# Output product by 32-row groups, and two sets of moments taken one stage earlier

## Reference, cut to what matters

```python
x = x + 0.5 * ffn(layernorm(x))     # 16 experts, the best 4 of each token, weighted
x = x + attention(layernorm(x))     # 16 heads of width 16, causal
x = x + 0.5 * ffn(layernorm(x))     # the same weights again
# layernorm(x) = (x - mean) / sqrt(var + 1e-5), no scale and no shift
# attention's end: sum over the heads of Z[b,h,s,:] @ WO  (16 x 256)  + 16 * bO
```

## Time and profile before

| what | us |
|---|---|
| median of 3 runs | 1567.58 (1565.57 to 1567.88) |
| the profiled execution, its own time | 1571.9 |
| its span | 1570.2 |
| PE busy | 1417.3 (90%) |
| PE weight loads busy | 960.6 (61%) |
| DVE busy | 1033.5 (66%) |
| ACT busy | 775.6 (49%) |
| POOL busy | 635.4 (40%) |
| mean granted clock of PE | 0.958 of 2.4 GHz |

### The profile page before, as it was taken

One profiled execution on the slowest core, in us unless ns is written; L12 is line 12 of the kernel. 1 busy time (PEld: TensorE's weight loads), 2 busy tenths in 40 slices (PEclk: granted clock), 3 DMA queues, 4 the chain that ended last, 5 costly groups with the idle time before them and its releaser, 6 DMA issues. The chain is left out here.

```text
span 1570.2 us, 32613 instructions
## 1 busy us (share of the span) xinstructions
PE 1417.3 (90%) x9764; PEld 960.6 (61%) x9764; DVE 1033.5 (66%) x2639; ACT 775.6 (49%) x1316; POOL 635.4 (40%) x676
## 2 busy tenths in 40 slices
PE   4899999999957769999999999999598999999997
PEld 3687888888846623333333343333276788888886
DVE  5675636366778768888788688884267564444667
ACT  4312666555125524665566466567351245655530
POOL 3371433766635460232222132222225406176764
PEclk9999999999979967999999999999879999999999
DMA  7741556888316920442334242200131227488873
GB/s 255 238 189 56 185 189 202 259 254 247 88 51 174 228 80 2 63 63 43 42 43 65 37 65 42 42 3 2 41 99 69 95 67 243 151 263 248 251 230 108
DMA packets 159221, 199.08 MB, mean 127 GB/s; under 512 B 18180, under 2 KB 132440, under 8 KB 159064
## 3 DMA queue, kind: packets, MB, share of 16 engines
q1 hardware_dynamic: 140632, 146.67, 35.0%
q0 software_dynamic: 18432, 50.36, 9.6%
HBM read 105.21 MB, written 91.49 MB: 125 GB/s over the span
## 5 line engine op out<-in xcount | busy, mean ns | idle before, releaser
L1579 ACT ACTIVATE attn_prob<-attn_b_ps 128x1024 f32<-128x1024 f32 (+3 forms) x352 | 304.0, 870 | 211.7 <-PE attn_b_ps L1752 210.7
L475 POOL DMA_INDIRECT xs_dram<-ffn_xn,ffn_index x192 | 188.0, 979 | 228.9 <-DVE ffn_index L745 172.6
L1732 PE MATMUL attn_a_ps<-k_rows,q_rows 96*128 96x512 bf16 (+3 forms) x768 | 250.5, 349 | 24.3 <-DVEq L1617 7.5
L489 POOL DMA_INDIRECT ffn_gathered<-ys_dram,ffn_index x192 | 195.6, 1019 | 89.9 <-issue 56.8
L1630 DVE TENSOR_REDUCE attn_max_a<-attn_a_ps 128x1 f32<-128x512 f32 (+2 forms) x304 | 202.5, 688 | 41.4 <-PE attn_a_ps L1732 22.7
L1523 POOL TENSOR_SCALAR_AFFINE_SELECT attn_prob<-attn_prob 128x512 f32<-128x512 f32 x128 | 81.3, 636 | 355.5 <-ACT attn_prob L1579 352.7
L789 DVE TENSOR_TENSOR ffn_xs_lo<-ffn_xt_ps,ffn_xs_hi 128x512 fp32r<-128x512 f32 x144 | 97.8, 679 | 156.4 <-ACT ffn_xs_hi L561 154.1
L1732 PEld LDWEIGHTS attn_a_ps<-k_rows,q_rows 96*128 96x128 bf16 x768 | 74.9, 98 | 190.1 <-DVE attn_max_a L1630 80.6
L1776 PE MATMUL attn_o_ps<-attn_prob,attn_v_now 128*17 128x256 f32 (+1 forms) x2560 | 189.0, 368 | 0.0
L1752 PE MATMUL attn_b_ps<-q_rows,k_rows 98*128 98x512 bf16 (+3 forms) x768 | 186.9, 331 | 0.3 <-ACT attn_prob L1579 0.3
L1627 DVE CUSTOM_DVE_ANT_0 attn_scored<-attn_a_ps,mask_wide 128x512 bf16<-128x512 f32 (+1 forms) x256 | 154.6, 623 | 40.5 <-PE attn_a_ps L1732 34.7
(11 more groups left out here) (199 smaller groups left out, 2729.5 us busy)
## 6 DMA issues: line engine op xcount, KB each, us to landing
ffn_xs<-xs_dram SPq DMA_DIRECT2D x138, 256.0 KB, 3.7
ys_dram<-ffn_y SPq DMA_DIRECT2D x138, 256.0 KB, 2.7
xs_dram<-ffn_y SPq DMA_DIRECT2D x16, 768.0 KB, 10.4
qk_parts<-proj_cut SPq DMA_DIRECT2D x32, 384.0 KB, 3.1
k_rows<-qk_parts SPq DMA_DIRECT2D x96, 128.0 KB, 4.5
q_rows<-qk_parts SPq DMA_DIRECT2D x96, 128.0 KB, 6.8
ffn_w_stage<-in_L_ffn_w_dram SPq DMA_DIRECT2D x64, 128.0 KB, 2.4
x_res<-in_L_attn_x_dram SPq DMA_DIRECT2D x4, 1024.0 KB, 8.5
```

The costliest lines, as they stand in the source:

```text
L475: pool.indirect_dma_start(xs_dram[(b + 1) % 2], bass.IndirectOffsetOnAxis(index[:, b, i, k:k + 1], 0), xn[:, b % 2, i, :], None, bounds_ch ...
L489: pool.indirect_dma_start(gathered[:, t % G_RING, k, :], None, ys_dram[b], bass.IndirectOffsetOnAxis(index[:, b, i, k:k + 1], 0), bounds_c ...
L1579: act.activation(prob[PROB[kt]][:, h:h + heads, prob_at(kt, kt * P):prob_at(kt, S)], b_ps[:, slot, :].rearrange("p (h t) -> p h t", h=head ...
L1732: ins = pe.matmul(a_ps[:, bank, i * keys:end], q_rows[q][0:SROWS, h0 + i, qt * P:(qt + 1) * P], k_rows[q][0:SROWS, h0 + i, first:first + k ...
```

## The change

Four things are done.

1. **Output product.** `wo_block` is replaced by `wo_rows` (128 x 256: wo and bo once in each 32-row strip) and a tile `o_zero` (128 x 512) that serves to clear `o_ps` in two copies. The four 512-column products of a batch become eight 256-column products, each of 32 rows of `z_t` with 32 rows of `wo_rows`, placed at row group 32j of the array. They come in pairs of strips: PE waits for both banks, then gives strip j and j+1 for the first tile, then for the second. A bank now holds tiles i and i+4 of the batch.
2. **Moments of the projection's first chunk.** A new class `ChunkMoments` takes over the statistics' tiles from `Norm` and lives through the program. Statistics of chunk 0 are taken by DVE in feed-forward 1 at slot step 45, the power by POOL between the gathers of batch 2 and 3, the Newton step by DVE behind the last slot.
3. **Projection's start.** DVE begins with apply(0). ACT cuts the first weight between the copies of tiles 1 and 2. The low parts of the three weights go from DVE to POOL, the memset of `v_res` goes behind apply(1).
4. **Moments of feed-forward 2's batch 0.** A class `Moments` holds the tiles of both feed-forwards. In the written-out last batch of attention DVE takes the statistics at group 2, step 17, POOL the power ahead of `head_sum` of group 2, DVE the Newton step at group 3, step 12. Feed-forward 2 has no statistics, power or Newton step for batch 0, and ACT's first normalize waits for nothing there.

```diff
@@ ffn, gpsimd
-            square_root(0)
+            if x_in is not None:
+                square_root(0)
             cut_weights(0)
             square_root(1)
...
             for b in range(1, BLOCKS):
                 gather(b)
+                if b == 2 and chunk is not None:
+                    chunk.pool_start(pool)
+                    chunk.pool_root(pool, 0)
@@ ffn, scalar
                 if i == 0:
-                    act.wait_ge(rstd_ready, b + 1)
+                    if b or x_in is not None:
+                        act.wait_ge(rstd_ready, b + 1 - made)
@@ ffn, vector
-            early_stats(0)
-            late_stats(0)
-            inverse_root(0)
             if x_in is not None:
+                early_stats(0)
+                late_stats(0)
+                inverse_root(0)
...
+                if n == MOMENTS_AT and chunk is not None:        # MOMENTS_AT = 45
+                    chunk.vector_stats(dve, steps, x_res, 0, range(CHUNK_TILES))
+            if chunk is not None:
+                chunk.vector_rstd(dve, steps, 0)
@@ project, scalar
             for j in range(CHUNK_TILES):
                 norm.scalar_copy(act, j, 0)
+                if j == 1:
+                    cut_weights(0)
             norm.scalar_hi(act, 0, 0)
-            for i in range(3):
-                act.wait_ge(w_loaded[i], 16)
-                act.activation(w_hi[:, i, :, :], w_stage[:, i, :, :], ACT.Copy).then_inc(w_hi_ready, 1)
+            cut_weights(1)
+            cut_weights(2)
@@ project, gpsimd
-            norm.pool_start(pool)
-            norm.pool_root(pool, 0)
-            norm.pool_root(pool, 1)
+            def cut_weights(i):
+                pool.wait_ge(w_hi_ready, i + 1)
+                pool.tensor_tensor(w_lo[:, i, :, :], w_stage[:, i, :, :], w_hi[:, i, :, :].bitcast(F32),
+                                   ALU.subtract).then_inc(w_lo_ready, 1)
+
+            cut_weights(0)
+            norm.ready.pool_root(pool, 1)
+            cut_weights(1)
+            cut_weights(2)
@@ project, vector
-            dve.memset(v_res[:, :, :, DH:DH + 1], 1.0)
...
-            stats(0)
-            apply(0)
+            dve.wait_ge(norm.xt_ready, 2)
+            norm.vector_apply(dve, x_res, 0, range(CHUNK_TILES))
             stats(1)
             norm.vector_lo(dve, 0, 0)
-            for i in range(3):
-                dve.wait_ge(w_hi_ready, i + 1)
-                dve.tensor_tensor(w_lo[:, i, :, :], w_stage[:, i, :, :], w_hi[:, i, :, :].bitcast(F32),
-                                  ALU.subtract).then_inc(w_lo_ready, 1)
             apply(1)
+            dve.memset(v_res[:, :, :, DH:DH + 1], 1.0)
@@ attention, gpsimd
-            pool.memset(wo_block[:, :, :], 0.0).then_inc(wo_zeroed, 1)
+            pool.memset(o_zero[:, :], 0.0)
+            pool.memset(wo_rows[:, :], 0.0).then_inc(wo_zeroed, 1)
...
+                    if last and q == ROOT_Q:                     # ROOT_Q = QUADS - 2
+                        square_root()
                     head_sum(b, q)
@@ attention, scalar
-            act.activation(o_ps[:, :], wo_block[:, :, :].rearrange("p j d -> p (j d)"), ACT.Copy).then_inc(o_zeroed, 1)
+            for i in range(S // HALF):
+                act.activation(o_ps[:, i * HALF:(i + 1) * HALF], o_zero[:, :], ACT.Copy).then_inc(o_zeroed, 1)
@@ attention, vector
-                    xs = x_res[:, bass.ds(b * QT + 2 * i, 2), :]
-                    dve.tensor_tensor(xs, xs, a_ps[:, bank, :].rearrange("p (j d) -> p j d", j=2),
+                    xs = x_res[:, bass.ds(b * QT, QT), :].rearrange("p (h j) d -> p h j d", h=2)[:, :, i, :]
+                    dve.tensor_tensor(xs, xs, a_ps[:, bank, :].rearrange("p (h d) -> p h d", h=2),
                                       ALU.add).then_inc(a_free, 1)
...
+                        if last and q == QUADS - 2 and n == AHEAD + 1:
+                            batch_stats(0)
+                            batch_stats(2)
+                            batch_stats(4)
+                            steps.then(batch_stats(6))
+                            batch_variance()
+                        if last and q == QUADS - 1 and n == LEAD:
+                            batch_rstd()
@@ attention, tensor
-                for i in range(QT // 2):
-                    bank, number = ring.take()
-                    pe.wait_ge(a_free, number + 1)
-                    pe.matmul(a_ps[:, bank, :], z_t[:, i // 2, :],
-                              wo_block[:, 2 * (i % 2):2 * (i % 2) + 2, :].rearrange("p j d -> p (j d)"),
-                              start=True, stop=True).then_inc(a_ready, 1)
+                for pair in range(0, QT // 2, 2):
+                    places = [(j, *ring.take()) for j in (pair, pair + 1)]
+                    for j, bank, number in places:
+                        pe.wait_ge(a_free, number + 1)
+                    for half in range(2):
+                        for j, bank, number in places:
+                            ins = pe.matmul(a_ps[:, bank, half * D:(half + 1) * D], z_t[32 * j:32 * j + 32, half, :],
+                                            wo_rows[32 * j:32 * j + 32, :], start=True, stop=True,
+                                            tile_position=(32 * j, 0))
+                            if half == 1:
+                                ins.then_inc(a_ready, 1)
```

More of the change, by code:

```diff
@@ L51 @@
 ROOT_AT = {1: 7, 2: 6}
+MOMENTS_AT = 45
 FIRST, SECOND, THIRD = 2, 13, 14
@@ L188, in three_passes, with __init__, sb, ffn @@
     return pe.matmul(out, a_hi, b_lo, start=False, stop=last)
+class Moments:
+    def __init__(self, nc, ctx):
+        def sb(n, shape):
+            return ctx.enter_context(nc.sbuf_tensor(f"moments_{n}", shape, F32))
+        self.stats = sb("stats", [P, BT, 6])
+        self.mv = sb("mv", [P, BT, 2])
+        self.veps = sb("veps", [P, BT])
+        self.power = sb("power", [P, BT])
+        self.root = sb("root", [P, BT])
+        self.fix = sb("fix", [P, BT])
+        self.rstd = sb("rstd", [P, 2, BT])
+        self.nmr = sb("nmr", [P, 2, BT])
 def tiles_of(n):
     return 1 if n % PAIRS == PAIRS - 1 and SLOT_TILES % 2 else 2
-def ffn(nc, name, nth, scattered, row_gathered, gate_t, x_in, x_res, ident, before_b, ones_b, gate_w, w1, w3, w2, xs_dram, ys_dram, out):
+def ffn(nc, name, nth, scattered, row_gathered, gate_t, moments, chunk, x_in, x_res, ident, before_b, ones_b, gate_w, w1, w3, w2, xs_dram, ys_dram, out):
     with ExitStack() as ctx:
@@ L328, in ffn @@
         stored = sem("stored")
+        made = 1 if x_in is None else 0
         last = stored.num
@@ L1306, in _, with attention @@
                 values(c, c % 2)
-def attention(nc, x_res, v_res, ident, ident_b, mask_wide, wo, bo, rows):
+def attention(nc, moments, x_res, v_res, ident, ident_b, mask_wide, wo, bo, rows):
     with ExitStack() as ctx:
@@ L1549, in _, with square_root @@
                 clear_masked(0, 0, kt, True)
+            def square_root():
+                pool.wait_ge(veps_ready, 1)
+                pool.tensor_tensor(moments.root[:, :], moments.veps[:, :], moments.power[:, :], ALU.pow).then_inc(root_ready, 1)
             at = steps.n
@@ L1909, in program @@
         gate_t = sb("gate_t", [P, KT, E], F32)
+        moments = Moments(nc, ctx)
+        chunk = ChunkMoments(nc, ctx)
         ident = sb("ident", [P, P], F32)
@@ L1927, in program @@
             norm_ctx.close()
[L1928 to L1929 removed]
+            attention(nc, moments, x_res, v_res, ident, ident_b, mask_wide, wo, bo, rows)
+        ffn(nc, "ffn2", 1, scattered, row_gathered, gate_t, moments, None, None, x_res, ident, before_b, ones_b, gate_w, w1, w3, w2, xs_dram, ys_dram, out)
 _INS = ["L0_attn_x", "L0_attn_WQ", "L0_attn_bQ", "L0_attn_WK", "L0_attn_bK", "L0_attn_WV", "L0_attn_bV",
```

125 lines of the change are left out of this document (75 added, 50 removed).

## The result

The changed kernel takes 1564.67 us in the median of 20 runs, against 1567.55 us for 20 runs of the kernel before on the same chip: ratio 0.9975, 95% interval 0.9963 to 0.9987. One of the 20 runs took 4572.14 us and stands in the median but not in the ratio; the other 19 have 1563.61. So the change brings 3.9 us by the ratio, where 8.9 was forecast: right in sign, less than half in size. The range ended at 1564.0, between the two medians. In two later comparisons the same kernel came to 0.9977 and 0.9967.

What follows compares the result with a forecast made beforehand. PE, busy 90% of the span, was taken to bound the kernel, losing share only at block borders. Terms -5.1 - 3.8 + 0.0 gave -8.9 us, from the median 1567.58 to 1558.7 us; range 1555.0 to 1564.0.

Steps and rivals of the forecast that it cites:

- Feed-forward 2's start, -5.1: Feed-forward 2's start: batch 0's moments leave the path, the weight cut and dense products come 5.1 us earlier, bounds 3.5 to 5.3.
- a bound for a late landing: Feed-forward 2's start: if the weight DMAs' landing takes 4.0 us, only 3.5 us are saved.
- Projection's start, -3.8: Projection's start: first dense product 4.3 us earlier, 0.5 given back, so 3.8 us saved, bounds 2.6 to 4.4.
- the 0.5 us for chunk 1: Projection: small DVE operations stretched beside POOL's cuts make chunk 1's tiles late for PE, giving 0.5 us back.
- Moved work at nothing: Attention's last batch and feed-forward 1: moved moments fit idle time, cost 0; in feed-forward 1 at most 0.7 us.
- Output product, 0.0 with bounds -0.8 and +1.8: Attention's output product: -0.1 us for each of three loop batches, +0.3 in the last, sum 0.0.
- the column groups: Output product: eight column-group instructions take 0.63 us, so row groups were taken to overlap likewise, a pair lasting one old product.
- PE passes its last wait about 0.2 earlier: Output product in loop batches: PE is done waiting about 0.2 us earlier though DVE ends 0.45 later; taken as -0.1 each.
- The DMAs take more of it: Rival at both starts: weights land late (1.6 and 1.2 less) or the clock rises late (1.3); -4.8, 1562.8 us, chance 0.11.
- No overlap of row groups: Rival at the output product: row groups do not overlap, a pair takes 0.87 us more; -5.5, 1562.1 us, chance 0.20.
- The clock stays low: Rival at both starts: half clock lasts into dense work; 25 us of it gives +3.6, 1571.2 us, chance 0.04.
- Drains: Output product: returning from row groups to whole products costs some 0.31 us a batch, 1.2 in all, within the bound.

Runs made afterwards that it cites:

- e11: Changed kernel with the output product strip by strip, plus useless products ahead of the last output product and at both starts; ratio 0.9963 to the kernel before.
- e18: Changed kernel with the old output product, PE waiting for both banks ahead of products one and three; 1562.08 us, ratio 0.9975 to the kernel before.
- e17: Changed kernel with the old output product, without the joint wait, measured a second time; 1557.17 us, ratio 0.9931 to the kernel before.
- e14: Changed kernel with the old output product and the joint wait for both banks, measured earlier than e18; ratio 0.9975 to the kernel before.
- e5: Changed kernel with the output product given strip by strip, PE waiting for one bank at a time; 1559.22 us, ratio 0.9937 to the kernel before.
- e15: Strip by strip as in e5, measured again beside the changed kernel on one chip; 1560.04 us, ratio 0.9945 to the kernel before.
- e13: Strip by strip as in e5, but PE waits for both banks ahead of each pair of strips; ratio 0.9974 to the kernel before.
- e3: Kernel before with only the output product changed to the new row groups; 1568.62 us, ratio 1.0022 to the kernel before.
- e12: e11 with 14 zero products more behind the output product of each loop batch; ratio 0.9944 to the kernel before.

## Why the prediction was wrong, point by point

- **Feed-forward 2's start, -5.1: right.** Alone -5.0 by the ratio. The block takes 434.3 to 439.9 us in the 17 executions with the moments taken earlier and 440.6, 443.0 and 444.5 in the three without. The DMA is late next, as said. Its landing moves the cut from 3.93 to 5.37 us behind the barrier, execution by execution, forecast 4.2; a bound for a late landing was needed (9.43 less 5.37 is 4.1 saved, bound 3.5), and the other execution lies past the upper bound (5.5 saved, bound 5.3).
- **Projection's start, -3.8: right.** Alone -4.4 by the ratio. The block takes 110.2 to 113.4 us in the 17 executions with the new start and 114.0, 116.8 and 118.3 in the three without. The first dense product moved by 4.83 (forecast 4.3), the small operations beside POOL lasted 1.24 and 1.20 us (1.09 in the earlier trace rows), and of the 0.5 us for chunk 1 only 0.18 went back. Chunk 1 came when forecast, 3.1 us behind PE's start, but PE had work at half clock until 2.9, where 2.7 was taken. That the half clock is what hides this wait shows in `e11`: 1.43 at full clock.
- **Moved work at nothing: right within what can be measured.** In attention the stretch from DVE's twelfth reciprocal (there is one for each of the 16 groups of heads) to the barrier takes 125.67 to 125.69 us in three executions of the old product with the moments in it, 125.63 and 125.73 in two without. Feed-forward 1 ends at 447.1, 450.4 and 454.4 us in three executions without them and between 443.9 and 453.8 in 17 with them; a cost of less than some us could not be seen in such a spread. POOL's memset and power lie in the gap ahead of the first gather of batch 3, of 5.57 us. It is 5.93 now (389.62 to 395.55), 0.4 longer, and still ended by DVE's sum, 4.67 behind POOL's last piece:

```profile
389.62 0.12 POOL L116 MEMSET chunk_power<- 128x4 f32 x1
389.83 1.04 POOL L122 TENSOR_TENSOR chunk_root<-chunk_veps,chunk_power 128x4 f32<-128x4 f32 x1
395.55 1.07 POOL L519 DMA_INDIRECT ffn_gathered<-ys_dram,ffn_index  x1 [4.67 <-DVE x_res L818]
```

  At slot step 45 DVE's next cut starts at 313.64, 2.37 behind its gate at 311.27, where the earlier trace rows has 1.79: 0.58 late, 0.6 was forecast.
- **Output product, 0.0 with bounds -0.8 and +1.8: the step that failed.** It was mis-sized by 3.4 to 5.6 us. The overlap was taken about rightly from the column groups (1.13 us for a pair of strips, one old product being half of 1.98), and the length of the last product too (6.86 us from its first product to the end of the last add, 6.41 to 6.57 in five executions of the old, forecast +0.3). The error is in the loop batches' part for PE: "PE passes its last wait about 0.2 earlier" counted PE's waits inside the product only. The wait of the next batch's first score product, which wants a bank of the same ring, was not counted, nor the one ahead of the first pair. The rows it was read from the earlier trace rows are of batch 0, where 3.80 us of the loop's turn follow and hide that wait; behind batch 2 no turn follows. So PE loses 0.96 us there instead of gaining 0.1; the times from the values' last products to the next batch at the first two turns are 7.54 in the mean of four executions of the new product against 7.43 of four of the old, 0.1 more each instead of 0.1 less. That the joint wait is what costs, and not the row groups, is shown by the old product with it: 4.9 us by the medians of `e18` and `e17`, more by their ratios. (The term's lower bound adds up to -0.7, not -0.8, which changes nothing.)
- **What of it the traces account for.** The third turn of the loop, from the twelfth reciprocal to the thirteenth, is 37.93, 37.94, 39.03 and 39.52 us with the new product (39.03 in the profile above) and 35.98 in five executions of the old. Of that 2.0 to 3.5 more, 0.96 is the waits and the rest a stretch at half clock that the old product doesn't have there. It isn't all loss: in three of the four the two last groups of heads are some 1.5 us shorter (46.2 to 46.3 against 47.7 to 47.9). From the twelfth reciprocal to the barrier, all in, it is 126.5, 126.6, 127.6 and 129.7 against 125.6 to 125.7: 0.8 to 4.0 more. `e18` has 126.2 and `e14` 127.8, 0.5 and 2.1 more; strip by strip it is 124.9 and 126.1, no loss in the mean, though their third turns are 36.96 and 38.14. So the half clock at the third turn does not mark the slow kernels.
- **The block as a whole.** Attention takes 559.1 to 561.8 us in five executions of the old product (mean 560.2) and 561.1 to 565.6 in four of the new (563.5); the old with the joint wait has 562.2 and 563.6. So most of the 3.4 to 5.6 us lies in this block, but the ranges touch, three executions of the changed kernel differ by 3 us among themselves, and how the waits' 1 to 2 us come to 3 and more is not shown.

The half clock behind the third turn's product, after and, in the second fence, before (columns of the earlier trace rows):

```profile
1009.10:1012.60 3.50, 2.62 (x15) 0.67 (x14) 2.42 (x6) 0.70 (x1) 0.00 (x0) 0.51 0.00 0
1012.60:1016.00 3.40, 3.40 (x26) 1.21 (x24) 1.82 (x5) 1.16 (x2) 0.00 (x0) 0.51 0.00 0
```

```profile
1011.30:1014.70 3.40, 3.11 (x26) 0.88 (x24) 2.86 (x9) 1.14 (x2) 0.00 (x0) 1.00 0.00 0
1014.70:1018.10 3.40, 3.37 (x42) 1.83 (x39) 2.61 (x7) 1.68 (x3) 0.37 (x1) 1.00 0.00 0
```

- **The rivals.** "The DMAs take more of it" gave 1562.8 and "No overlap of row groups" 1562.1; both are nearer to the time than the forecast, and both for reasons that the runs do not bear out: the starts alone are worth 4.4 and 5.0 us, and a pair of strips does overlap. "The clock stays low" was to be decided at the starts, and there it rose as before. The mean clock did fall, from 0.959 or 0.960 to 0.956, but `e5` shows the same fall without the loss.
- **Drains.** The Trainium skill, "TensorEngine Tiling (Array Packing)", section Key Properties, has a change of tiling mode drain TensorE, which was priced at some 0.3 us a batch. Strip by strip goes into row groups and out again and takes 4.60 to 4.62 us at the third turn in three executions where the old product takes 4.62; in a fourth (`e15`), where half clock sets in during the product, it takes 5.19. At full clock no price of a drain shows. The same page, section Restrictions and Gotchas, says that different row tiles cannot access one PSUM bank at the same time; it is why a pair needs two banks and so a joint wait. A pair that shares a bank was not tried on the chip.

## What beats both

The old product with the two sets of moments (1556.45 and 1557.17 us, 0.9941 and 0.9931) and the row groups strip by strip (1559.22 and 1560.04, 0.9937 and 0.9945) are both faster than the kernel before, and by their ratios than the changed one (beside it on one chip only `e15`). The second needs only the edit of `e5` in `output` and keeps the smaller tiles.

## What to carry to other kernels

A ring of two buffers keeps two engines busy only as long as each waits for one buffer at a time; an operation that takes both turns it into a relay, and its length is then the sum. Here the second pair starts 2.64 us behind the first: 1.13 of products, 1.28 of adds and the handing over. When a step's waits are compared, follow the ring past the step: the first user behind it waits for the same buffers. And price a loop's step at each of its turns, since the last has no turn of the loop behind it to hide in.

## What was not expected of the hardware

- Products of two row groups went side by side in either order: 1.13 us when the groups alternate (the change), 1.14 when both products of one group stand ahead of those of the other (`e13`).
- Kernels with products by row group and no fill have a lower mean clock than those with the old product, 0.956 against 0.961 to 0.962 (`e3` 0.953, the kernel before beside it 0.960), some 18 us more at half clock in a span of 1560, with or without the joint wait. It did not show in the time.
- Between kernels the mean clock told nothing of the time: 0.966 and 1559.12 us (`e12`), 0.956 and 1559.22 us (`e5`).
- The same four weight DMAs at feed-forward 2's start kept ACT idle for 4.05 us in one execution and 2.62 in another of the same kernel.
- Feed-forward 1, whose code is the same in all kernels but for the small moments moved into it, ended between 443.9 and 454.4 us in twenty executions. A difference of that kind between two profiles says nothing of the change.
